# A graph attention layer on one core: fifteen of the sixteen early value tables move from VectorE and ScalarE to GpSimd

## The reference

```python
Wh = (x @ W.T).reshape(n, 4, 32)
score_l = einsum('nhd,hd->nh', Wh, a_l); score_r = einsum('nhd,hd->nh', Wh, a_r)
e = leaky_relu(score_l[:, :, None] + score_r.T[None, :, :], 0.2)
e = where(adj + eye > 0, e, -inf)          # mask, the same for all heads
out = elu(einsum('nhm,mhd->nhd', softmax(e, axis=2), Wh).reshape(n, 128))
y = layernorm(x + out)
```

## Time and profile before

| | us |
|---|---|
| median of 3 runs | 1793.12 (1792.2 to 1793.35) |
| the profiled execution | 1793.73 |
| its span, first to last instruction | 1791.9 |
| DVE, ACT, PE, POOL busy | 1685.0, 1667.2, 1651.9, 26.2 |

### The profile page before, as it was taken

How to read it: one execution, slowest core, us unless ns; L and a number is a source line. 1 busy time by engine, 2 the same in 40 slices (tenths; PEclk the granted TensorE clock), 3 DMA queues, 4 the chain that set the end, 5 groups by cost and what they waited for, 6 DMA issues and landing times. The chain is left out here.

```text
span 1791.9 us, 80971 instructions
## 1 busy us (share of the span) xinstructions
PE 1651.9 (92%) x37067; PEld 1628.6 (91%) x37067; DVE 1685.0 (94%) x1903; ACT 1667.2 (93%) x1248; POOL 26.2 (1%) x36
## 2 busy tenths in 40 slices
PE   7698888999899999999999999999999999999995
PEld 6688788899899999999999999999999898999995
DVE  4999999998989989999998989999899999999997
ACT  3999999889899999999999999998999999999992
POOL 0000000000001000000000100000000100000000
PEclk9899999999999999999999999999999999999998
DMA  7996787999999786675766676666767131111111
GB/s 231 349 352 220 270 279 261 331 314 329 308 305 315 244 265 192 207 242 184 239 208 215 202 237 199 219 212 209 229 191 244 34 83 56 39 58 37 34 37 36
DMA packets 241476, 368.10 MB, mean 205 GB/s; under 512 B 12912, under 2 KB 103408, under 8 KB 239600
## 3 DMA queue, kind: packets, MB, share of 16 engines
q1 hardware_dynamic: 241136, 362.92, 62.3%
HBM read 345.57 MB, written 17.30 MB: 203 GB/s over the span
## 5 line engine op out<-in xcount | busy, mean ns | idle before, releaser
L494 ACT ACTIVATE bmask<-lrow,rtab 128x2048 fp8e4<-128x2048 f32 (+1 forms) x977 | 1544.4, 1662 | 9.4 <-PE psum L403 8.6
L403 PE MATMUL psum<-vring,cmask 128*128 128x99 bf16 x14336 | 718.6, 208 | 42.5 <-DVE cmask L721 33.2
L403 PE MATMUL psum<-vring,bmask 128*128 128x99 bf16 x14336 | 720.5, 208 | 10.1 <-DMA vring<-v_scratch 5.1
L403 PEld LDWEIGHTS psum<-vring,cmask 128*128 128x128 fp8e4 x14336 | 661.4, 98 | 55.7 <-DVE cmask L721 43.7
L403 PEld LDWEIGHTS psum<-vring,bmask 128*128 128x128 fp8e4 x14336 | 668.5, 97 | 12.4 <-issue 6.2
L716 DVE SCALAR_TENSOR_TENSOR bmask<-acache,bmask 128x1024 int32<-128x1024 int32 x512 | 624.2, 1219 | 50.1 <-ACT bmask L494 44.7
L721 DVE SCALAR_TENSOR_TENSOR cmask<-acache,bmask 128x1024 int32<-128x1024 int32 x512 | 623.2, 1217 | 3.0 <-PE psum L403 3.0
L697 DVE TENSOR_SCALAR bmask<-lrow,rtab 128x2048 fp8e4<-128x2048 f32 (+1 forms) x303 | 315.3, 1054 | 0.0
L372 PE MATMUL trp<-pack,abuf 128*128 128x64 bf16 x4096 | 143.1, 193 | 22.8 <-issue 12.9
L372 PEld LDWEIGHTS trp<-pack,abuf 128*128 128x128 bf16 x4096 | 131.7, 98 | 24.8 <-issue 22.7
L463 ACT CAST acache<-trp 128x512 int16<-128x512 f32 x128 | 73.9, 577 | 56.8 <-PE trp L372 56.5
(11 more groups left out here) (64 smaller groups left out, 268.4 us busy)
## 6 DMA issues: line engine op xcount, KB each, us to landing
abuf<-in_adj_dram SPq DMA_DIRECT2D x256, 1024.0 KB, 8.3
vring<-v_scratch SPq DMA_DIRECT2D x384, 99.0 KB, 3.2
lrow<-l_scratch SPq DMA_DIRECT2D x16, 1024.0 KB, 7.7
v_scratch<-vt SPq DMA_DIRECT2D x16, 792.0 KB, 11.1
vring<-v_scratch SPq DMA_DIRECT2D x64, 198.0 KB, 6.7
cmask<-in_x_dram SPq DMA_DIRECT2D x16, 256.0 KB, 5.0
late<-in_x_dram SPq DMA_DIRECT2D x16, 256.0 KB, 5.3
out_dram<-late SPq DMA_DIRECT2D x16, 256.0 KB, 3.6
```

Source lines behind the costliest of these rows:

```text
L403: return nc.tensor.matmul(psum[:, bank, at * S3:(at + 1) * S3], mask[:, j * P:(j + 1) * P], values, start=opening, stop=True, skip_group_c ...
L494: last = nc.scalar.activation(to, rows, ACT.Relu, bias=rtab[:, 2 * s + i, H + h:H + h + 1], scale=BIG, saturate=False)
```

## The change

Table 0 is made as before, by DVE and ACT. Tables 1 to 15 are made by POOL alone, in a loop behind its constants and ahead of its small row work: the same six operations on the same buffers, each waiting for the one before through the same semaphores. DVE and ACT lose their calls and nothing is put in their place. What waits for a table (PE, `store_v`, `load_v`, `evacuate`) waits for the same semaphore values.

```diff
@@ ScalarE
-            highest(1)
...
-                if q % EVERY_STEPS == 1 and q // EVERY_STEPS + 1 < JUST_MADE * NG:
-                    middle(q // EVERY_STEPS + 1)
-                if q % EVERY_STEPS == 3 and q // EVERY_STEPS + 2 < JUST_MADE * NG:
-                    highest(q // EVERY_STEPS + 2)
@@ VectorE
-            weigh(1)
...
-                if q % EVERY_STEPS == 0 and q // EVERY_STEPS + 1 < JUST_MADE * NG:
-                    rest(q // EVERY_STEPS + 1)
-                if q % EVERY_STEPS == 2:
-                    if q // EVERY_STEPS + 1 < JUST_MADE * NG:
-                        lowest(q // EVERY_STEPS + 1)
-                    if q // EVERY_STEPS + 2 < JUST_MADE * NG:
-                        weigh(q // EVERY_STEPS + 2)
@@ GpSimd
+            def table(n):
+                h, g = 2 * (n // NG), n % NG
+                slot = vt[:, n % VS].rearrange("p u t b e -> p (u t b) e")
+                pool.wait_ge(vv_done, 2)
+                if n < NG:
+                    pool.wait_ge(wh_copied, 4 * (g + 1))
+                pool.wait_ge(v_rest, n)
+                pool.wait_ge(v_hi, n)
+                w4 = wh[:, G * g:G * g + G, h * E:(h + 2) * E].rearrange("p t (u e) -> p u t e", e=E)
+                v5 = vf.rearrange("p (u t b) e -> p u t b e", u=2, b=2)
+                for b in range(2):
+                    vb = vv[:, G * g:G * g + G, h:h + 2, b].rearrange("p t (u o) -> p u t o", o=1).to_broadcast([P, 2, G, E])
+                    last = nc.gpsimd.tensor_tensor(v5[:, :, :, b], w4, vb, ALU.mult)
+                last.then_inc(v_prod, 1)
+                pool.wait_ge(v_prod, n + 1)
+                if n >= VS:
+                    pool.wait_ge(v_out[n % VS], 16 * (n // VS))
+                    pool.wait_ge(mm_done, EVERY_STEPS * (n - VS + 1))
+                nc.gpsimd.tensor_copy(slot[:, :, 0:E], vf).then_inc(v_hi, 1)
+                pool.wait_ge(v_hi, n + 1)
+                pool.wait_ge(v_mid, n)
+                pool.wait_ge(v_lo, n)
+                nc.gpsimd.tensor_tensor(vr, vf, slot[:, :, 0:E], ALU.subtract).then_inc(v_rest, 1)
+                pool.wait_ge(v_rest, n + 1)
+                nc.gpsimd.tensor_copy(slot[:, :, E:2 * E], vr).then_inc(v_mid, 1)
+                pool.wait_ge(v_mid, n + 1)
+                nc.gpsimd.tensor_tensor(slot[:, :, 2 * E:S3], vr, slot[:, :, E:2 * E], ALU.subtract).then_inc(v_lo, 1)
+
+            for n in range(1, JUST_MADE * NG):
+                table(n)
```

More of the change, by code:

```diff
@@ L463, in evacuate, with highest, middle @@
                 nc.scalar.copy(acache[:, c % 2, half, m].bitcast(i16), trp[:, :]).then_inc(evac_done, 1)
[L465 to L477, removed]
+            def highest():
+                act.wait_ge(v_prod, 1)
+                nc.scalar.copy(vt[:, 0].rearrange("p u t b e -> p (u t b) e")[:, :, 0:E], vf).then_inc(v_hi, 1)
+            def middle():
+                act.wait_ge(v_rest, 1)
+                nc.scalar.copy(vt[:, 0].rearrange("p u t b e -> p (u t b) e")[:, :, E:2 * E], vr).then_inc(v_mid, 1)
             def compare(q):
@@ L515, in _ @@
             evacuate(1)
-            highest(0)
+            highest()
             copy_l()
-            middle(0)
+            middle()
             compare(1)
             compare(2)
-            highest(1)
             for q in range(Q):
@@ L620, in _, with weigh, rest, lowest @@
             copy_l(NC - 1)
[L622 to L630, removed]
+            def weigh():
+                dve.wait_ge(vv_done, 2)
+                dve.wait_ge(wh_copied, 4)
+                w4 = wh[:, 0:G, 0:2 * E].rearrange("p t (u e) -> p u t e", e=E)
                 v5 = vf.rearrange("p (u t b) e -> p u t b e", u=2, b=2)
                 for b in range(2):
-                    vb = vv[:, G * g:G * g + G, h:h + 2, b].rearrange("p t (u o) -> p u t o", o=1).to_broadcast([P, 2, G, E])
+                    vb = vv[:, 0:G, 0:2, b].rearrange("p t (u o) -> p u t o", o=1).to_broadcast([P, 2, G, E])
                     last = nc.vector.tensor_tensor(v5[:, :, :, b], w4, vb, ALU.mult)
                 last.then_inc(v_prod, 1)
[L637 to L646, removed]
+            def rest():
+                dve.wait_ge(v_hi, 1)
+                nc.vector.tensor_tensor(vr, vf, vt[:, 0].rearrange("p u t b e -> p (u t b) e")[:, :, 0:E], ALU.subtract).then_inc(v_rest, 1)
+            def lowest():
+                dst = vt[:, 0].rearrange("p u t b e -> p (u t b) e")
+                dve.wait_ge(v_mid, 1)
                 nc.vector.tensor_tensor(dst[:, :, 2 * E:S3], vr, dst[:, :, E:2 * E], ALU.subtract).then_inc(v_lo, 1)
@@ L831, in mean_part @@
                                                ALU.mult, ALU.mult).then_inc(nmr_done, 1)
-            weigh(0)
+            weigh()
             add_diagonal(0, 0)
             add_diagonal(0, 1)
-            rest(0)
+            rest()
             compare(0)
             mask_b(0)
-            lowest(0)
+            lowest()
             compare(1)
             mask_c(0)
-            weigh(1)
             for q in range(Q):
```

## The result

The changed kernel took 1848.2 us (median of 4, 1847.4 to 1850.1) against 1793.2 us before on the same chip: ratio 1.0293, 95% interval 1.0262 to 1.0325, so 55 us slower. The forecast was 1873 us, in a range of 1780 to 1912. The profiled execution has a span of 1846.5 us against 1791.9.

What follows compares the result with a forecast made beforehand. The prediction took DVE's and POOL's time in the first two passes as one bound: 256 - 6.4 - 53.7 + 15 x 9.3 = 335.4 us, +79.4. With +1 for the last table, +80 gave 1873 us, range 1780 to 1912.

Steps and rivals of the forecast that it cites:

- The bound of the stretch: First two passes, 48 to 304 us: POOL's reading time and DVE's time add up to one bound, 335.4 us.
- the 6.4 us that I let POOL use: First two passes: DVE's idle time, 6.4 us of 256, counted as usable by POOL and subtracted from the sum.
- What goes: Tables 1 to 15: two multiplies and two subtractions each leave DVE, 53.7 us; two casts each leave ACT, 30 us.
- Exclusion in both directions: First two passes: DVE's masks and compares keep POOL out, and POOL's instructions likewise hold up DVE; stretch 79.4 us longer.
- POOL's price to DVE: POOL's six instructions a table: 9.3 us without fixed parts, floor 5.2, ceiling 12.7; 15 tables.
- a cheaper POOL: POOL's table making: 7.1 us a table would give +47 us, 1840 us; 5.2 us only +18 us.
- PE's clock: PE in the first two passes: idling may lower its clock, but 118 us of room; cost 0, up to +15 us.
- The last table's round trip: End of the second pass: last table stored and loaded back before step 64; between -1.9 and +3 us, taken as +1.
- A sign to look for: PE's waits in the first two passes should name vt by POOL, the last difference, at PEclk below 0.99.
- The first: Rival: POOL's long instructions don't hold up DVE and POOL keeps up; 1777 us, at most 30 us faster; chance 0.18.
- The second: Rival: DVE never held up, POOL waits at each of six instructions, 18.3 us a table; +35 us, 1828 us; chance 0.13.
- The third: Rival: POOL's delay and ACT's gain cancel, or DMA and PE set the same 16 us; 1793 us; chance 0.05.

Runs made afterwards that it cites:

- the one-part runs: Kernel before, with only the products, only the casts or only the subtractions of tables 1 to 15 moved to GpSimd: 1798.8, 1816.5 and 1810.4 us.
- the writes-only run: Changed kernel with each of GpSimd's six instructions a table replaced by a memset of the same output, nothing read: 1779.7 us, against 1795.5 before.
- the two runs without reads: Changed kernel with GpSimd's six instructions a table replaced by five one-column writes (1782.9 us) or by memsets of the same outputs (1779.7 us); before 1795.5.

## Why the prediction was right, and where it was off

- **The bound of the stretch** was read rightly: DVE and POOL as one bound, ACT (236 us of 315) and PE (239) below it. DVE's idle time was 7.9 us from 48 to 310.5 us before and 7.5 us from 48 to 363 us after, so the 6.4 us that I let POOL use were not used: an error of 6 us.
- **What goes** (53.7 us on DVE) was right by the one-part runs, whose sums close with it to 10 us.
- **Exclusion in both directions** was the step that the rows could show only from one side, and it gave the sign. It holds: masks of 2.12 and 3.13 us beside POOL's instructions, and 117 us lost where POOL read beside an unchanged kernel. The Trainium skill's rule ("SBUF — State Buffer", section "Who interferes with whom") had the exclusion, and also that a two-input VectorE instruction minds only GpSimd instructions that read; the writes-only run agrees with this (masks 1219 and 1215 ns). That the pair is held for the whole instruction is a little more than was measured: masks paid 0.2 us less than POOL's shortest length.
- **The mis-sized term** was POOL's price to DVE: 9.3 us a table forecast, 7.1 measured, 15 x 2.2 = 33 us too much. I priced a two-input element at 2.2 ns and a one-input one at 1.1. The instructions' own length was 2 us a table shorter (10.5 us forecast with the fixed parts; shortest seen: subtraction 2.11 us, cast 1.10 us, product 1.10 us, together 8.6 us), and what DVE pays was less again, 1.68, 0.81 and 0.74 us: 0.2 us less for each of six instructions would be 7.4 us, and some fall where DVE pays nothing. The 2.2 ns was picked between 1.1 and 3.0 from instructions of 8 to 128 elements, so its size was an estimate, and the prediction's own test failed it: a product of 1.2 to 1.5 us and a subtraction of 2.2 to 2.8 were to show the price right, and both were below. From +80 us: -33 for the price, +6 for the idle time, is +53; measured +55. The prediction's own list named a cheaper POOL as the way down, and this lies on it. The stretch ended at 363 us, 315 us long, where about 340 was expected; masks and compares grew by 94 us in sum, where 100 or more was.
- **PE's clock** was costed at 0 and this held as far as the runs show: the mean granted clock fell from 0.97 to 0.90 in the stretch, PE had 76 us to spare, and its waits name DVE.
- **The last table's round trip** was to cost 1 us: PE waited 2.24 us for vring, 1.92 before.
- **A sign to look for was wrong.** I expected PE to wait for the last subtraction of POOL. POOL had its tables ready early and waited 64.5 us for free slots; the loss reached PE through the masks. In a shared bound the one whose buffers fill first stops, and the other's product is what is late.
- **The rivals.** The first (no hold on DVE) would have given 1777 us; the two runs without reads show that its size was right, 1780 and 1783, and its premise wrong. The second asked that DVE not be held up and PE wait for tables; neither is so. The third, no change, is ruled out by the 55 us.

## What to carry to other kernels

Before work goes to GpSimd, take the undisturbed length of each of its instructions that reads, and charge VectorE that length less 0.2 us where VectorE is full of instructions like these masks and compares. If no length is known, count the elements read from all inputs, at the 0.7 to 1.0 ns seen here. In a kernel bound by VectorE the move pays only if VectorE gives up more than that. Here a two-input VectorE instruction of 1056 elements gave back 1.17 us and cost 1.68, and a cast taken from ScalarE gave VectorE nothing back and cost it 0.81 us. An engine that is idle isn't free: look in the trace for its small instructions in the busy part and for the same ones in a quiet part (1.08 against 0.29 us here) before counting on it.

## What the runs showed of the hardware that was not expected

GpSimd's writes alone leave VectorE's two-input masks untouched (1213 to 1219 ns beside 83 and 91 us of memsets) and lengthen only the fast compares (894 and 992 ns up to the first product from vring, against 748). GpSimd can also be kept out for long: one cast of 1056 elements, 1.10 us at its shortest, took 9.85 us from 199.08 us on in the changed kernel, while seven masks of DVE in a row, from 199.95 us on, kept their normal length. It ended when DVE had stood idle for 0.98 us, waiting for PE. Four of the seven, what DVE did next, and POOL:

```profile
201.09 1.22 DVE L697 SCALAR_TENSOR_TENSOR bmask<-acache,bmask 128x1024 int32<-128x1024 int32 x1
202.22 1.21 DVE L702 SCALAR_TENSOR_TENSOR cmask<-acache,bmask 128x1024 int32<-128x1024 int32 x1
...
205.63 1.22 DVE L697 SCALAR_TENSOR_TENSOR bmask<-acache,bmask 128x1024 int32<-128x1024 int32 x1
206.77 1.22 DVE L702 SCALAR_TENSOR_TENSOR cmask<-acache,bmask 128x1024 int32<-128x1024 int32 x1
208.96 3.85 DVE L708 TENSOR_REDUCE acc<-psum 128x165 f32<-128x495 f32 x7 [0.98 <-PE psum L403]
```
```profile
199.08 9.85 POOL L934 CAST vt<-vring 128x1056 bf16<-128x1056 f32 x1 [7.74 <-PE psum L403]
209.01 2.11 POOL L938 TENSOR_TENSOR late<-vring,vt 128x1056 f32<-128x1056 f32 x1
```

Who gets in at a boundary is thus not always decided in turn; nothing here tells what decides it.
